# Repairing a failed top-32 scan with three passes of eight instead of four (gated cross-attention, two layers, one Trainium2 core)

## The reference, cut to what matters

```python
# L1_xattn: q, k, v split into 16 heads; scores are [batch, head, 256, 1601]
scores = jnp.einsum('bhqd,bhkd->bhqk', q, k) / SCALE
top_scores, top_idx = jax.lax.top_k(scores, 32)
w = jax.nn.softmax(top_scores, axis=-1)
top_v = jnp.take_along_axis(v[:, :, None, :, :], top_idx[..., None], axis=3)
out = jnp.einsum('bhqk,bhqkd->bhqd', w, top_v)
```

## Time and profile before

| | us |
|---|---|
| median of 3 runs | 5451.87 |
| lowest and highest | 5446.61, 5455.07 |
| the profiled execution, its own time | 5462.37 |
| span of the profiled execution | 5460.3 |
| TensorE busy | 4684.1 (86%) |
| VectorE busy | 4361.7 (80%) |
| ScalarE busy | 4036.6 (74%) |
| GpSimd busy | 1154.4 (21%) |

### The profile page before, as it was taken

How to read it: one execution, slowest core, us unless ns; L and a number is a source line. 1 busy time by engine, 2 the same in 40 slices (tenths; PEclk the granted TensorE clock), 3 DMA queues, 4 the chain that set the end, 5 groups by cost and what they waited for, 6 DMA issues and landing times. The chain is left out here.

```text
span 5460.3 us, 110204 instructions
## 1 busy us (share of the span) xinstructions
PE 4684.1 (86%) x34502; PEld 2229.0 (41%) x34502; DVE 4361.7 (80%) x23240; ACT 4036.6 (74%) x5196; POOL 1154.4 (21%) x2648
## 2 busy tenths in 40 slices
PE   4878788999798889979989999997999799988776
PEld 2434334353343435334343544434353344434222
DVE  4458888878878797897879888788878888887772
ACT  1457677878687697868869788886878688787763
POOL 2121122222122222212212222222222122121110
PEclk7889899999899899989989999998999899999886
DMA  4232222223122132322313222231323223121110
GB/s 119 69 73 54 59 62 54 70 59 80 49 62 72 43 80 57 76 54 62 75 38 80 55 73 71 62 74 47 74 60 77 52 60 71 36 65 30 34 26 19
DMA packets 356337, 332.23 MB, mean 61 GB/s; under 512 B 102074, under 2 KB 313149, under 8 KB 355711
## 3 DMA queue, kind: packets, MB, share of 16 engines
q1 hardware_dynamic: 355710, 324.84, 24.3%
HBM read 217.54 MB, written 107.13 MB: 59 GB/s over the span
## 5 line engine op out<-in xcount | busy, mean ns | idle before, releaser
L942 DVE MAX8 cand<-s 128x8 f32<-128x67 f32 (+1 forms) x12288 | 1988.3, 222 | 116.8 <-ACT s L894 67.5
L913 ACT ACTIVATE prob<-wide 128x1024 f32<-128x1024 f32 (+1 forms) x1792 | 1778.7, 1025 | 390.2 <-PE wide L635 188.8
L1028 DVE TENSOR_REDUCE part<-score 128x1 f32<-128x512 f32 (+1 forms) x2048 | 1122.3, 564 | 395.4 <-PE score L594 264.1
L681 PE MATMUL att<-prob,v 128*9 128x256 f32 (+1 forms) x14336 | 1110.3, 389 | 27.9 <-ACT prob L913 26.1
L635 PE MATMUL wide<-q,k_att 128*128 128x256 bf16 (+1 forms) x6656 | 1023.4, 281 | 103.9 <-ACT s L894 56.2
L894 ACT ACTIVATE s<-wide 128x1024 f32<-128x1024 f32 (+1 forms) x1024 | 843.1, 845 | 309.6 <-DVEq L1082 174.5
L903 ACT ACTIVATE below<-wide 128x1024 bf16<-128x1024 f32 (+1 forms) x832 | 828.2, 1024 | 131.6 <-PE wide L635 123.5
L594 PE MATMUL score<-k_scan,q 128*128 128x512 bf16 (+1 forms) x2048 | 666.3, 349 | 220.9 <-DVE part L1028 178.7
L635 PEld LDWEIGHTS wide<-q,k_att 128*128 128x128 bf16 (+1 forms) x6656 | 583.3, 101 | 562.5 <-ACT s L894 149.5
L1271 POOL TENSOR_SCALAR flag<-cand,ends 128x24 bf16<-128x24 f32 x512 | 178.6, 349 | 2494.4 <-DVE ends L967 2243.5
L657 PE MATMUL wide<-below,minus_ident 128*128 128x512 bf16 (+1 forms) x1664 | 504.5, 386 | 97.2 <-ACT below L903 86.2
(11 more groups left out here) (161 smaller groups left out, 5202.2 us busy)
## 6 DMA issues: line engine op xcount, KB each, us to landing
k_scan<-k_stack SPq DMA_DIRECT2D x512, 150.1 KB, 2.6
k_stack<-split_b SPq DMA_DIRECT2D x576, 128.0 KB, 2.4
k_att<-k_stack SPq DMA_DIRECT2D x384, 192.0 KB, 3.3
ctxT<-in_ctx_dram SPq DMA_DIRECT2D x32, 800.5 KB, 5.2
q_stack<-split_b SPq DMA_DIRECT2D x192, 64.0 KB, 2.1
q<-q_stack SPq DMA_DIRECT2D x128, 96.0 KB
self_stack<-split_b SPq DMA_DIRECT2D x192, 64.0 KB, 2.1
k_self<-self_stack SPq DMA_DIRECT2D x64, 96.0 KB
```

What stands on the lines that cost most here:

```text
L681: r = tensor.matmul(att[32 * j:32 * j + HD + 1, 0:S], v[0:kc, c, j0 * HG + j, :], m.prob[n % 3][0:kc, j * S:(j + 1) * S], start=(c == 0), ...
L913: scalar.activation(pr[0:kc, :], ps[0:kc, :], ACT.Exp, scale=SCALE).then_inc(sem["wide_done"], 1)
L942: i = vector.max(cand[:, :, c], s[:, KCUT[c]:KCUT[c + 1]])
L1028: vector.tensor_reduce(m.part[:, QT * hh + qt, c:c + 1], score[i % 2][:, 0:wd], AX.X, ALU.max).then_inc(sem["score_max"], 1)
```

## The change

In the repair, the first of the four MAX8 of each tile is left out. What it wrote is already in the same place, `ends[:, ..., 0, :]`, from the merge (L960). The first instruction of a tile's repair is now the MATCH_REPLACE8 that strikes these eight out of `s`. So three MATCH_REPLACE8 and three MAX8 are left of seven passes over 1601 columns, and the wait between the first MAX8 and the first MATCH_REPLACE8 goes with the MAX8.

```diff
@@ -1071,11 +1071,10 @@
                                 s, ends = m.s[(tile + n) % 4], m.ends[g % 2]
                                 best = [ends[:, QT * pair + n, 0, :], m.top_again[:, 0, :], m.top_again[:, 1, :],
                                         ends[:, QT * pair + n, 1, :]]
-                                for i in range(TOPK // 8):
-                                    if i:
-                                        vector.match_replace(s[:, :], best[i - 1], s[:, :], NEG).then_inc(redo, 1)
-                                        steps += 1
-                                        vector.wait_ge(redo, steps)
+                                for i in range(1, TOPK // 8):
+                                    vector.match_replace(s[:, :], best[i - 1], s[:, :], NEG).then_inc(redo, 1)
+                                    steps += 1
+                                    vector.wait_ge(redo, steps)
                                     vector.max(best[i], s[:, :]).then_inc(redo, 1)
                                     steps += 1
                                     vector.wait_ge(redo, steps)
```

## The result

| | before | after |
|---|---|---|
| median, us (4 executions each) | 5452.2 | 5411.7 |
| lowest and highest | 5446.6, 5455.1 | 5407.2, 5413.9 |
| the profiled execution, its own time | 5462.4 | 5413.9 |
| mean granted clock in it | 0.936 | 0.944 |

The ratio is 0.9927 (95% interval 0.9916 to 0.9939): 40.5 us less. The forecast was 29.8 us less. Timed again with five more executions, the changed kernel came to 5405.3 us, ratio 0.9911 (0.9897 to 0.9925). Either more came off the repairs than forecast, or something else happened besides; the traces say which.

What follows compares the result with a forecast made beforehand. No engine is full; each repair is a full stop of the core set by VectorE's chain of passes. Eight repairs of 3.72 us less make 29.8 us, other terms 0: 5451.87 to 5422.1 us, range 5409 to 5437 us.

Steps and rivals of the forecast that it cites:

- A repair is a full stop, set by VectorE's passes.: In each of eight repairs VectorE works alone for about 26.75 us; two MAX8 less take off 3.72 us.
- Nothing else becomes late.: At a repair's end, ScalarE and TensorE start 3.72 us sooner, whole; no other work or DMA hides the saving.
- The first MATCH_REPLACE8 costs no more to start than the MAX8.: Right behind the branch into the repair: start cost taken as 0, between +2.7 and -0.7 us over eight repairs.
- The sum, 29.8 us.: Eight repairs, each 3.72 us shorter by two MAX8, take 29.8 us off the median of 5451.87 us.
- The jumps over the block, taken as 0 with -3 to +3 us.: For the 248 pairs that pass the test, skipping a block two instructions shorter changes nothing, bound -3 to +3 us.
- The clock within 0.002 of 0.936.: TensorE's mean granted clock over the changed kernel's run stays within 0.002 of 0.936.
- The rival of the vanishing relapses.: TensorE's low-clock stretches behind repairs 4 and 6 vanish, up to 10.8 us more off, 5411 us; chance 6%.
- The price of the lower level, up to 0.32 us for each us.: A 16.6 us relapse of TensorE's clock behind a repair costs up to 5.4 us, 0.32 us per us.
- 85% of it nowhere near a repair: Of 699 us that the core spends at TensorE's lower clock level, 85% lies nowhere near a repair.
- that the clock's window runs free of the program: TensorE's activity is judged in a free-running window, so relapses would be redrawn in any execution, not by this change.

Runs made afterwards that it cites:

- three other doses: Kernel before with first MAX8 cut to 8 columns: 5425.1 us; with two more MAX8 a tile: 5511.2 us; with first MAX8 left out for second tile only: 5432.3 us.
- half of the change: Against the kernel before, the first MAX8 is kept for a pair's first tile and left out for the second: 5432.3 us, ratio 0.9961.
- the code in four other places: Changed kernel plus never-entered branch with one MAX8, 5420.7 us, or 24, 5423.9 us; plus eight MEMSETs at VectorE's start, 5418.5 us, or sixteen, 5427.0 us.
- the kernel with two rows of dead code: Changed kernel plus a never-entered inner branch holding one small MAX8 at the end of the repair: 5420.7 us, ratio 0.9947.
- the repair per tile: Contains the change; marks are summed so that inside the branch each tile is repaired only if its own marks are not zero: 5353.6 us, ratio 0.9817.

## Why the prediction was right or wrong

- *A repair is a full stop, set by VectorE's passes.* Right. The stop shrank by 3.72 us eight times, with ScalarE's wait following to within 0.02 us, and two of the three other doses gave what the passes weigh (-25.7 us for 26.8 forecast, +60.3 for 59.7). The third, half of the change, gave -18.5 for 14.9, with the code moved too.
- *Nothing else becomes late.* Right: leaving the repair out gives back 0.94 to 1.03 times the stops.
- *The first MATCH_REPLACE8 costs no more to start than the MAX8.* Right, 0.64 us in both.
- *The sum, 29.8 us.* Right for the passes, too small for the whole: 40.5 us in the first timing, about 43 us over nine executions. The time lies in the range, but below the forecast's own range (5413 to 5431). What came on top of the 29.8 us was luck in where the code happened to stand, not something the change brings by itself: with the same stops and the code in four other places, the gain is 20.4 to 28.9 us.
- *The jumps over the block, taken as 0 with -3 to +3 us.* This is the term that was mis-sized. It looked only at the waits behind the jumps, which did shrink by 3.2 us. It read them from a mean of 0.83 and a longest of 1.1 us as standing close together, "as a jump of fixed cost would have it". One by one they are two groups, 195 near 0.76 us and 53 near 1.07 us. It also left out that shorter code also moves all code behind it, and that this changes the time outside the stops by anything between -13 and +6 us against the 5236.5 us of the kernel before: 5223.6 as the changed kernel stands, 5234.0, 5236.3, 5239.5 and 5242.5 us in the four kernels with the same stops and other places of the code.
- *The clock within 0.002 of 0.936.* Wrong: 0.944, and the kernel before itself was at 0.943 in its next profile. One execution's clock was no base for such a bound.
- *The rival of the vanishing relapses.* It gave 5411 us, the measured median, for the wrong reason. The relapses come and go in the kernel before as well; in both profiles of the kernel before the median is the same 5450 us and only the execution differs. On the other hand it was right that executions of one kernel differ by 15.8 us and that the clock is the likeliest reason, only too small: the next eleven executions spread over 27 us.
- *The price of the lower level, up to 0.32 us for each us.* It fits the 0.28 us between executions of one kernel. But "85% of it nowhere near a repair" is wrong: of the 697 us at the lower level in that profile, 171.5 us, a quarter, lie inside the eight stops alone. No term of the sum rests on it.
- *The Trainium skill, "TensorE: Matmul & The Clock Gate", Part 1:* that the clock's window runs free of the program, so that the return is earlier or later from run to run. The two executions of the same kernel agree with the second half of this: behind repair 4 the clock came back 4.5 us after the repair's end and then relapsed in one, and came back after 10.7 us without a relapse in the other. That the window is what makes the difference, no run here shows.
- What stays open is how the code's place reaches the clock. The traces show that the wait behind a jump is some 0.31 us longer in some cases, and in others of the 248 when the code moves (at the check that ends at 448 us, 1.12 us before and 0.76 us after). They also show that the sum of these waits doesn't decide: the kernel with two rows of dead code has the shorter waits and the longer time. Whether a few of them stand where a slightly later start of TensorE makes its clock fall, or other fetches of code play a part, no run here tells apart.

## What to carry to other kernels

Where every other engine shows zero busy time up to the end of a stretch, the work in it is worth its full length, and a sum of instructions by durations was exact here for the stretch itself; look then for whether the work is needed at all, as the repair per tile shows (98 us under the kernel before). Before a remainder of 0.2% is explained by a mechanism, profile the same kernel twice and shift its code by a few instructions: both moved this kernel's time by more than the remainder. A profile of one execution gives durations, but not the clock of the next execution.

## What the runs showed that I had not expected

- Instructions that never run, or run once at the start, changed the median by 10 to 19 us of 5420 (0.2 to 0.35%). Single executions lie within 4 to 10 us of the median of their kernel, those of the kernel before within 14 us, so it takes medians of several to see this.
- The idle time behind a conditional jump was mostly 0.76 us, and some 0.31 us more in 24 to 101 of 248 cases in the kernels with a repair, nearly the same cases each time for the same code.
- Apart from the clock, executions repeat closely: the 215 stretches between checks in which two executions of the same kernel had about the same time at the lower clock differed by 0.7 us in their sum, over a span of 5.4 ms.
